# Expert rows at fixed places, tokens routed in three groups, and the last sums made by TensorE, in a kernel of alignment and experts

## What is computed

```python
x = x + align(ctx_1024, layernorm(x))       # dynamic time warping of 77 rows onto 512 tokens, rows summed along the path
x = x + ffn(layernorm(x), ...)
def ffn(x, ...):                            # T = 2048 tokens, H = 128, I = 512, E = 8 experts, K = 2
    scores = sigmoid(xf @ gate_w + bias)
    top_scores, top_idx = top_k(scores, K)
    top_scores = top_scores / (sum(top_scores) + 1e-06)
    w = zeros((T, E)).at[token, top_idx].add(top_scores)
    hact = gelu(einsum('th,ehi->tei', xf, up_w) + up_b)
    eo = einsum('tei,eih->teh', hact, down_w) + down_b
    combined = einsum('teh,te->th', eo * 0.1, w)
    shared = (gelu(xf @ sw_up + sb_up) @ sw_down + sb_down) * 0.1
    out = shared + combined
    return out / (max(abs(out), axis=-1) + 1e-06)
```

## Time and profile before

| what | us |
|---|---|
| median of 3 runs | 290.02 (288.14 to 290.07) |
| time of the profiled execution | 287.41 |
| its span, first to last instruction | 285.7 |
| busy: DVE, PE, ACT, POOL | 193.9, 161.6, 128.6, 112.5 |
| mean granted clock of PE | 0.770 |

### The profile page before, as it was taken

The page is one execution under the profiler, slowest core; times in us unless marked ns, Lnnn a source line. Parts: engine busy times, 40 slices in busy tenths (PEclk is TensorE's granted clock), DMA queues, the critical chain, the costliest instruction groups (busy, mean ns, idle before and its releaser), DMA issues. The chain is left out here.

```text
span 285.7 us, 5134 instructions
## 1 busy us (share of the span) xinstructions
PE 161.6 (57%) x1262; PEld 108.3 (38%) x1263; DVE 193.9 (68%) x926; ACT 128.6 (45%) x323; POOL 112.5 (39%) x210
## 2 busy tenths in 40 slices
PE   1690089991000014663478995099999999982000
PEld 0330034430000013642322331069999999972000
DVE  3843999999955816856539690058888888860590
ACT  5550049950003032295076421058888888850020
POOL 8100030000000023030477777325888888874540
PEclk9997559998555555555579999559999999999555
DMA  7013999994330000000011111222333323101922
GB/s 202 2 40 83 134 317 331 204 181 69 65 61 7 1 0 2 2 1 0 20 56 49 47 47 55 66 58 78 92 84 91 92 77 98 39 3 27 267 73 73
DMA packets 39747, 22.83 MB, mean 80 GB/s; under 512 B 14796, under 2 KB 36787, under 8 KB 39719
## 3 DMA queue, kind: packets, MB, share of 16 engines
q1 hardware_dynamic: 36824, 17.98, 27.3%
q0 software_dynamic: 2496, 4.24, 4.5%
q10 hardware_dynamic: 399, 0.28, 0.3%
HBM read 12.51 MB, written 10.89 MB: 82 GB/s over the span
## 5 line engine op out<-in xcount | busy, mean ns | idle before, releaser
L646 POOL DMA_INDIRECT expert_dram<-arena_d,result_place x46 | 47.8, 1039 | 14.7 <-issue 12.1
L793 ACT ACTIVATE arena_f<-bank,tile_bias 128x256 f32<-128x256 f32 x92 | 36.3, 474 | 3.4 <-PE bank L939 2.6
L937 PE MATMUL bank<-down_hi,arena_d 128*128 x184 | 32.8, 220 | 1.0 <-DVE arena_g L1302 1.0
L938 PE MATMUL bank<-arena_a,up_hi 128*128 128x256 f16 (+1 forms) x108 | 33.1, 307 | 0.0
L1302 DVE TENSOR_TENSOR arena_g<-arena_f,arena_d 128x512 f16<-128x512 f32 x46 | 31.8, 692 | 1.6
L939 PE MATMUL bank<-down_hi,arena_g 128*128 x184 | 32.6, 219 | 0.0
L938 PE MATMUL bank<-down_lo,arena_d 128*128 x184 | 32.6, 219 | 0.0
L605 POOL COPY met_at<-arena_b 32x3 f16 (+1 forms) x26 | 3.9, 181 | 67.6 <-DVE arena_b L1145 63.4
L1085 DVE TENSOR_TENSOR_SCAN arena_b<-arena_c,edge,arena_a 64x33 f32<-64x33 f32 x92 | 25.6, 278 | 4.7 <-DMA arena_a<-dist_dram 4.6
L884 PE MATMUL bank<-arena_b,minus_one 128*128 (+1 forms) x26 | 3.9, 185 | 43.1 <-issue 43.1
L937 PE MATMUL bank<-arena_d,up_hi 128*128 128x256 f16 x92 | 26.1, 284 | 0.5 <-DVE arena_a L1294 0.5
(11 more groups left out here) (232 smaller groups left out, 443.5 us busy)
## 6 DMA issues: line engine op xcount, KB each, us to landing
sorted_dram<-padding SPq DMA_DIRECT2D x1, 2990.0 KB, 20.6
arena_g<-sorted_dram SPq DMA_DIRECT2D x23, 130.0 KB, 2.1
arena_d<-in_L_ffn_up_w SPq DMA_DIRECT2D x6, 256.0 KB, 4.7
arena_d<-in_L_ffn_down_w SPq DMA_DIRECT2D x5, 256.0 KB, 5.2
x_sb<-in_x SPq DMA_DIRECT2D x4, 256.0 KB, 4.4
arena_b<-expert_dram SPq DMA_DIRECT2D x4, 256.0 KB, 4.0
arena_c<-expert_dram SPq DMA_DIRECT2D x4, 256.0 KB, 4.4
out<-x_sb SPq DMA_DIRECT2D x4, 256.0 KB, 2.3
```

Source lines behind the costliest of these rows:

```text
L646: pool.indirect_dma_start(out=expert_dram.ap(), in_=y_row[:, j % Y_SLOTS, n, :], in_offset=None, out_offset=bass.IndirectOffsetOnAxis(ap=p ...
L793: last = act.activation(hid[:, k, m, cols], banks[UP_BANK + HALVES * k + m][:, cols], ACT.Gelu, bias=bias, scale=1.0 / WSCALE)
L937: pe.matmul(o, a_hi, b_hi, start=start, stop=False)
L938: pe.matmul(o, a_hi, b_lo, start=False, stop=False)
```

## The change

- **Fixed places.** Expert e's rows begin at row 2048 e of a `sorted_dram` of 16,640 rows, so that a row's slot needs no count of tiles. Unused room stays padding; a table `tile_row` gives each of the 23 tiles its first row, and SP reads it into a register before each load.
- **Padding** is now written by ACT's queue, issued after the first two weight pieces, from 13 rows held in `x2`: 1,280 runs of 6,760 bytes, 8.65 MB in place of 3.06. ACT waits for it before it first writes `x2`, POOL before its first scatter.
- **Three groups.** Batch 0, batch 1 and batches 2 and 3 are routed one after the other. `first_row` carries the rows used so far. Scatters go out by group: 4 + 4, 4 + 4, 8 + 8. The programs of DVE, ACT and PE around it are put in a new order; the copy of batch 3 to `row_and_place2` stands between the second and the third group on POOL. The tables of tiles are computed after the slots.
- **Gates** are turned once, as one 128x128 transpose; their product with the experts' down biases moves to the tail, against a block matrix `bias_of_tile` that is cleared by DVE and filled by 16 small DMAs on SP's queue. The shared bias is added by ACT. PE no longer waits for the gates or the slots before the shared expert.
- **Tail.** The eight loads are issued four by SP and four by ACT; PE adds gates times biases, shared part and both choices in PSUM; DVE finds the peaks, ACT scales all 16 tiles, DVE adds `x2`, and `result` has its own buffer for each batch.

The diff, cut to its core:

```diff
+CAPACITY = B * S
+PAD_ROW = E * CAPACITY
+FILL_ROWS = 13
+ROUTED = (0, TPB), (TPB, 2 * TPB), (2 * TPB, TILES)
...
-        sorted_dram = nc.dram_tensor("sorted_dram", (EXPERT_TILES * ET, H + 2), F32, kind="Internal")
+        sorted_dram = nc.dram_tensor("sorted_dram", (PAD_ROW + ET, H + 2), F32, kind="Internal")
...
-            sp.wait_ge(ffn_const_ready, 1)
-            pads = sorted_dram.ap().rearrange("(j p) d -> p j d", p=P)
-            sp.dma_start(pads, padding[:].unsqueeze(1).to_broadcast([P, EXPERT_TILES * PARTS, H + 2])
-                         ).then_inc(zeroed, 16)
...
+                first = sp.value_load(tile_row[0:1, j:j + 1], min_val=0, max_val=PAD_ROW)
+                sp.dma_start(x_row[:, k], sorted_dram.ap()[bass.ds(first, ET), :].rearrange("(p n) d -> p n d", n=PARTS)
+                             ).then_inc(x_row_in[k], 16)
+
+            sp.wait_ge(table_ready, 2)
...
+                if j == SLOTS:
+                    sp.wait_ge(bias_cleared, 1)
+                if j < SLOTS + TILES:
+                    t = j - SLOTS
+                    sp.dma_start(bias_of_tile[t * E:(t + 1) * E, t * H:(t + 1) * H], down_b).then_inc(bias_in, 16)
...
+            for i, (t0, t1) in enumerate(ROUTED):
+                if i == len(ROUTED) - 1:
+                    second_copy(B - 1)
+                for k, src in enumerate((row_and_place, row_and_place2)):
+                    pool.wait_ge(slots_ready, TOP * i + k + 1)
+                    if k:
+                        pool.wait_ge(second_rows, 1 + max(t1 // TPB, B - 1))
+                    for t in range(t0, t1):
+                        pool.indirect_dma_start(
+                            out=sorted_dram.ap(), in_=src[:, t, :], in_offset=None,
+                            out_offset=bass.IndirectOffsetOnAxis(ap=slot[:, k, t:t + 1], axis=0)
+                        ).then_inc(scattered, 16)
...
-                pool.tensor_tensor(by_token[0][:, cols], by_token[0][:, cols], by_token[1][:, cols], ALU.add
-                                   ).then_inc(pair_ready, 1)
...
+                if n == 2:
+                    act.wait_ge(ffn_const_ready, 1)
+                    act.dma_start(pads, padding.unsqueeze(1).to_broadcast([P, each // FILL_ROWS, FILL_ROWS * (H + 2)])
+                                  ).then_inc(zeroed, 16)
...
+            deviation(0)
+            normalise(0)
+            deviation(1)
+            normalise(1)
+            turned_high(0)
+            deviation(2)
+            deviation(3)
+            squash(0)
+            normalise(2)
+            turned_high(1)
+            normalise(3)
+            turned_high(2)
+            squash(1)
+            turned_high(3)
+            squash(2)
+            act.wait_ge(zeroed, 16)
...
+            read_results(act, 1)
             for b in range(B):
-                if POOL_TILES[b]:
-                    act.wait_ge(tail, 2 * b + 2)
-                    if b >= 2:
-                        act.wait_ge(out_done[b % 2], 16 * (b // 2))
-                for n in range(TPB - POOL_TILES[b], TPB):
-                    act.activation(result[:, b % 2, n, :], total[:, b % 2, n, :], ACT.Copy,
-                                   scale=inv_peak[:, b, n:n + 1]).then_inc(scaled_by_act, 1)
+                act.wait_ge(tail, 2 * b + 2)
+                for n in range(TPB):
+                    last = act.activation(result[:, b, n, :], summed(b * TPB + n), ACT.Copy, scale=inv_peak[:, b, n:n + 1])
+                last.then_inc(scaled_by_act, 1)
...
+            turn_batch(0)
+            turn_batch(1)
+            ask_gate(0)
+            turn_batch(2)
+            count_rows(0)
+            ask_gate(1)
+            turn_batch(3)
+            count_rows(1)
+            ask_gate(2)
+            ask_gate(3)
+            count_rows(2)
...
-                pe.matmul(o, down_b_all[:], gatesT[:, b * S:(b + 1) * S], start=True, stop=False)
...
+                    if b == 0:
+                        pe.wait_ge(gates_ready, 1)
+                        pe.transpose(banks[GATES_BANK][:, 0:TILES * E], gates[:].rearrange("p n e -> p (n e)"), ident[:]
+                                     ).then_inc(gatesT_in_psum, 1)
...
+            pe.wait_ge(gatesT_ready, 1)
+            pe.wait_ge(bias_in, 16 * TILES)
+            for b in range(B):
+                pe.matmul(banks[b][:], gatesT[:], bias_of_tile[:, b * S:(b + 1) * S], start=True, stop=False)
+                for t in group_list(b):
+                    pe.matmul(summed(t), accT[:, t * P:(t + 1) * P], ident[:], start=False, stop=False)
+            for b in range(B):
+                pe.wait_ge(by_token_in[b], 16 * TOP)
+                for k in range(TOP):
+                    mm = pe.matmul(banks[b][:], ident[:], by_token[k][:, b * S:(b + 1) * S], start=False,
+                                   stop=k == TOP - 1)
+                mm.then_inc(total_in_psum, 1)
...
+            def choose(i):
+                t = slice(*ROUTED[i])
+                dve.wait_ge(score_ready, i + 1)
...
+            def place_rows(i):
+                t0, t1 = ROUTED[i]
+                t, n = slice(t0, t1), t1 - t0
+                o = banks[RANK_BANKS[i]]
+                dve.wait_ge(ranks_in_psum, i + 1)
+                routed(dve.tensor_tensor_scan(running[i][:].rearrange("p e n -> p (e n)"),
+                                              carry_on[i][:].rearrange("p e n -> p (e n)"),
+                                              o[:, E * n:2 * E * n], 0.0, ALU.mult, ALU.add))
+                routed(dve.tensor_tensor(offset[i][:], o[:, 0:E * n].rearrange("p (e n) -> p e n", e=E), running[i][:],
+                                         ALU.add),
+                       lambda: dve.tensor_tensor(first_row[:, i + 1], first_row[:, i], running[i][:, :, n - 1], ALU.add
+                                                 ).then_inc(aside_ready, 1))
+                routed(dve.tensor_tensor(place[:, t].rearrange("p n e -> p e n"), each_tile(first_row[:, i], n),
+                                         offset[i][:], ALU.add))
+                routed(dve.tensor_tensor(part[:, 0, t], pick[:, 0, t], place[:, t], ALU.mult),
+                       lambda: dve.tensor_tensor(part[:, 1, t], pick[:, 1, t], place[:, t], ALU.mult
+                                                 ).then_inc(aside_ready, 1))
+                with nc.allow_low_precision(reason="one whole number and zeros"):
...
+            hold(0)
+            trace(0)
+            hold(1)
+            trace(1)
+            hold(2)
+            trace(2)
+            sum_stats(0)
+            hold(3)
+            spread(0)
+            trace(3)
+            sum_stats(1)
+            spread(1)
+            sum_stats(2)
+            sum_stats(3)
+            turned_low(0)
+            spread(2)
+            spread(3)
+            keep_logits(0).then_inc(logits_ready, 1)
+            choose(0)
+            place_rows(0)
+            turned_low(1)
+            keep_logits(1).then_inc(logits_ready, 1)
+            turned_low(2)
+            choose(1)
+            place_rows(1)
+            turned_low(3)
+            keep_logits(2)
+            keep_logits(3).then_inc(logits_ready, 1)
+            choose(2)
+            place_rows(2)
...
+            routed(dve.tensor_tensor(skipped[:], past[0:1], unused[0:1].unsqueeze(1).to_broadcast([1, EXPERT_TILES, E]),
...
+            routed(dve.scalar_tensor_tensor(tile_row_f[:], tile_no[0:1], float(ET), tile_row_f[:], ALU.mult, ALU.add))
+            dve.tensor_scalar(tile_row[:], tile_row_f[:], float(PAD_ROW), None, ALU.min).then_inc(table_ready, 1)
...
+            dve.memset(bias_of_tile, 0.0).then_inc(bias_cleared, 1)
...
+            def add_x2(b):
+                dve.wait_ge(scaled_by_act, b + 1)
+                dve.tensor_tensor(result[:, b], result[:, b], x2[:, batch_tiles(b), :], ALU.add).then_inc(result_ready, 1)
+
+            for b in range(B):
+                find_peak(b)
+                if b:
+                    add_x2(b - 1)
+            add_x2(B - 1)
```

More of the change, by code:

```diff
@@ L758, in _, with deviation, normalise @@
-            act.wait_ge(logits_ready, 1)
-            act.activation(score[:], logits[:], ACT.Sigmoid).then_inc(score_ready, 1)
-            for b in range(1, B):
+            def deviation(g):
+                t = batch_tiles(g)
+                act.wait_ge(var2_ready, g + 1)
+                act.activation(sd[:, t], mv[:, t, 1], ACT.Sqrt, bias=eps[:]).then_inc(sd2_ready, 1)
+            def normalise(g):
+                act.wait_ge(shift_ready, g + 1)
+                for t in group_list(g):
+                    last = act.activation(y[:, t, :], summed(t), ACT.Identity, bias=shift[:, t:t + 1],
+                                          scale=rstd[:, t:t + 1])
+                last.then_inc(y2_ready, 1)
@@ L761, in _ @@
+            deviation(1)
[13 more added lines that the diff above has]
+            for b in range(B):
                 keep_sum(b)
-            act.wait_ge(gatesT_in_psum, 1)
```

(31 more changed lines are left out.)

316 lines of the change are left out of this document (127 added, 189 removed).

## The result

The changed kernel took 280.62 us (median of 4 runs, 279.30 to 281.44); the kernel before, on the same chip, 289.41 (4 runs, 288.14 to 290.07). The ratio is 0.970, with a 95% interval of 0.964 to 0.975: faster by 3%, and 1.3 us over the forecast of 279.3. The profiled execution took 280.42 us, of which 278.3 is its span; before it was 285.7. The profiled executions differ by less (7.0 us) than the medians (8.8), since the one before lay 2.0 us under its median and the one after 0.2. So 7.4 us of span have to be found in the traces.

A forecast was written before the change was run, and what follows sets the result against it. POOL's chain of scatters was taken to set the time from 139 to 185 us. A first tile 7.8 us earlier (8.9 - 0.6 - 0.5) plus 2.9 in the tail gave 10.7, so 279.3 us, range 276 to 286.5.

The forecast's parts named there:

- three signs of being wrong: POOL's third group waits for slots, the rows of choices are late, or the first scatter does not move.
- First scatter, -8.9: POOL's first scatter, after routing batch 0 alone, begins at 130.2 instead of 139.07, 8.9 us earlier.
- 0.9 from the slot to POOL's start: Last step to the first scatter: POOL starts 0.9 us after the slot, as in the kernel before.
- No gap, +0.6: POOL's 32 scatters run on at 1.33 us each without waiting for slots; one copy between groups adds 0.6.
- The fourth rival, scatters slowed by DVE: Twelve scatters beside the routing take 1.49 us each, costing 6.2 us, so 285.5; chance 8%.
- Register read, +0.5: SP's register read before the first tile load adds 0.5 us, bounds 0.3 and 1.1.
- Under it, 0: PE's shared expert and DVE's table work stay hidden before the first tile's rows; no gain or cost.
- Padding, 0: In the front, the 8.65 MB of padding lands near 75, before choice rows are wanted at 88.67; cost 0.
- the second rival: Padding holds up the front: choice rows return 3 to 8 us late, taken as 5, so 284.3; chance 14%.
- Tail, -2.9: From the last result scatter to the end, the new order of loads and sums saves 2.9 us.
- 1.7 us is shorter than any idle time seen to lose it: Argument against a cold tail: PE idles only from 256.4 to 258.1 and so keeps its clock.
- The rival's +7: Cold tail: PE's clock falls and the eight sums take 1.8 us each, +7, so 286.3; chance 12%.

The follow-up runs named there:

- e10: The changed kernel with 40 already-met waits put into POOL's program long before the walk; 277.93 us, ratio 0.966 to the kernel before.
- e12: The changed kernel with the changes of e9, e10 and e8 together, plus 12 unread matmuls in PE's tail; 273.29 us, ratio 0.950.
- e8: The changed kernel with SP reading the first two tiles' rows into registers before its wait for the last scatter; 278.79 us, ratio 0.967.
- e11: The changed kernel with the changes of e9, e10 and e8 together; 274.61 us, ratio 0.951.
- e6: The kernel before, with POOL's five result tiles in the tail given to DVE; 285.11 us, ratio 0.986.
- e9: The changed kernel with `above_first` moved from SP's queue to ACT's, ahead of the padding; 275.80 us, ratio 0.955.
- e2: The changed kernel with the padding issued behind ACT's reads of the choices, on a slower chip; DVE's mark came at 121.87, 5.4 us later.
- e3: The same kernel as e10, run on a slower chip and read only up to the first scatter, which began at 132.69.
- e4: The changed kernel with POOL's copy of batch 2 moved behind the first two scatter groups, on a slower chip; first scatter at 131.81.

## Why the prediction was right, and where it was right by luck

The forecast of 279.3 us and its range held, and the main argument did: the chain of scatters set the time, it could start as soon as one batch had its slots, it ran on without a gap, and the experts' stage did not change. But 3.3 us of the forecast 10.7 did not come in the traces, and errors hid each other. Most of the marks that the prediction had set were missed: the first scatter came at 134.84 (130 to 131), the last ended at 177.58 (173 to 174), PE waited 9.2 us for the first tile (5 to 7), and the last rows came 17.68 us behind the last result scatter (10 to 15). Of its three signs of being wrong one came, late rows of choices.

- **First scatter, -8.9.** Right in its mechanism and, but for a stall that I could not see, in its size: mark to scatter is 16.19 us in e10 and e12, and 25.17 less 8.9 is 16.3. The changed kernel lost 2.1 of it between slots and scatter. The step that failed is "0.9 from the slot to POOL's start": it took 3.0.
- **No gap, +0.6.** The chain took 42.74 for 42.60, in spite of its copy of 0.62. The fourth rival, scatters slowed by DVE, did not come: of the eight that began before the third group's slots were made, all but the first took 0.96 to 0.97. The first took 1.18, as the first of before (1.17), and two later ones 1.48 and 1.49, beside casts and splits of 512 columns. The Trainium skill, "SBUF — State Buffer", section Who interferes with whom, has a DVE operation with two inputs in SBUF contend only with GpSimd instructions that read SBUF, and infers that making DMA descriptors needs the write side; my rival left that restriction out. The trace agrees with the page: the scatters beside the routing's small operations (mostly 4 to 64 elements) were not slower.
- **Register read, +0.5.** The stretch grew by 1.0 us, 0.75 of which e8 took back. It was inside its bounds, 0.3 to 1.1.
- **Under it, 0.** Right in that it cost nothing: PE ended the shared expert at 172.9 (171.5 forecast), and waited 9.2 us for the tile.
- **Padding, 0.** Wrong by 2.6 us. The padding's end was near (71.3 for 75, as the rate was 410 to 422 GB/s and not 326). The step that failed is "the rows of choices are wanted at 88.67, so the cost is 0": it looked at the padding's own end and not at what stood on the other queue beside it. That was the second rival, a little below its lowest price of 3. The Trainium skill, "DMA: Bandwidth & Descriptors", section Queues, rings and completion order, has the DMA engines take turns between queues a packet at a time. The trace agrees in that the other queue slowed: with 6,760-byte runs on ACT's queue, two weights on SP's went from about 1 us of issue to 6.0 and 2.2; the turns themselves are not seen. Where rule and row could not be compared, I should have given the rule more than 14%.
- **Tail, -2.9.** In four of six profiles 15.5 to 15.8 us, 2.4 to 2.7 less than before; in the changed kernel's own and in e11's the clock fell, and only 0.5 were left. "1.7 us is shorter than any idle time seen to lose it" was right, but the idle time was 2.05 to 2.50, because the first pair landed 4.0 to 4.5 us after its issue and not 3.7. That was the term of the sum that was mis-sized. The rival's +7 was too high, as three of the eight sums were slowed and not all. No run tries the tail's new arrangement by itself; its 2.4 to 2.7 us are read from the traces.
- **Exit, not in the sum.** 3.85 us of gain, from POOL's drain. The rows were there in the trace of before, and I had taken the last 6.5 us of the span as fixed, without saying so. e6 shows the cause on the kernel before. Without this gain the profiled spans would differ by 3.6 us only.

So the forecast was near because -3.85 that nobody had counted stood against +2.6, +2.1 and +2.4 that were missed. The 3.3 us that are left shrank to 1.3 because the forecast had added 2.6 us for the step from the profiled execution to the median, and in the changed kernel that step was 0.2. Both are luck.

## What to carry to other kernels

A bulk transfer that is hidden by its own end isn't free: list what is issued on the other queues while it runs, and let small transfers that a chain waits for go first, which gave back 3 us here (e9); and look for engines that read registers while it flows. Look at the last instructions of the program as at any stage: an engine with slow housekeeping at its end should get its last work early, which was worth 3 to 4 us here for one constant (e6). When an engine starts late and its releaser is "issue", nothing in the data will explain it; shifting its program by some harmless instructions is a cheap test.

## What the hardware showed that was not expected

- A register read by DVE took 0.30 us in a quiet stretch and 1.0 to 1.1 us while the padding flowed, with 417 GB/s from 92 to 98 us and 380 from 98 to 110 (e2).
- POOL started 2.1 us later than it could, with one 8 KB packet of an instruction queue as the only traffic, 2.0 to 2.1 us ahead of the start in all six traces with the stall; 40 more instructions far ahead, or a few fewer, took this away (e3, e10, e4).
- POOL's drain at the end of the program lasted 7.0 to 8.4 us in all three shapes of the tail (up to 9.9 on the slower chip), and ended 6.4 to 6.5 us behind POOL's last work in all fourteen traces.
- While writes in runs of 6,760 bytes were in flight, all transfers together went at 410 to 422 GB/s, and 417 in e2 without the weights beside them; the earlier trace rows has 204 with runs of 520.
- On one chip the four kernels and the kernel before took some 10% more. In the four traces the experts' stage took 27 to 36 us longer, while the marks (but e2's) and the chains of scatters (41.8 to 43.8 us) were about as on the others; ACT waited up to 7.7 us for a signal whose sender the profile doesn't name (e4). Its cause is open.
